# Cross-attention of a decoder layer: the next group's rows are normalised, turned and split during the output projection, and the batch turn runs in another order

## What is computed

```python
# H = 16 heads, DK = DV = 64, DIM = 512
q_i = _split_heads(q @ Wq, H)              # q = _layernorm(x)
k_i = _split_heads(k @ Wk, H)              # k = v = ctx_1024, (2, 128, 512)
v_i = _split_heads(v @ Wv, H)
s_qk = jnp.einsum('...hik,...hjk->...hij', q_i, k_i) / jnp.sqrt(DK)
s_qk = jnp.where(mask, s_qk, neg)
attn = jax.nn.softmax(s_qk, axis=-1)
vals = jnp.einsum('...hij,...hjv->...hiv', attn, v_i)
x = x + _merge_heads(vals) @ Wo
```

## Time and profile before

| | us |
|---|---|
| median of three runs (lowest, highest) | 2826.04 (2825.84, 2826.16) |
| the profiled execution, its own time | 2824.46 |
| its span in the trace | 2822.8 |
| PE busy in the span | 2761.5 (98%) |
| DVE, ACT, POOL busy in the span | 1783.8 (63%), 1592.6 (56%), 1063.0 (38%) |

### The profile page before, as it was taken

How to read it: one execution, slowest core, us unless ns; L and a number is a source line. 1 busy time by engine, 2 the same in 40 slices (tenths; PEclk the granted TensorE clock), 3 DMA queues, 4 the chain that set the end, 5 groups by cost and what they waited for, 6 DMA issues and landing times.

```text
span 2822.8 us, 46193 instructions
## 1 busy us (share of the span) xinstructions
PE 2761.5 (98%) x13287; PEld 2279.2 (81%) x13289; DVE 1783.8 (63%) x2600; ACT 1592.6 (56%) x2748; POOL 1063.0 (38%) x692
## 2 busy tenths in 40 slices
PE   7999999999999999999999999999999999999998
PEld 6888888888878888788778888887788888888886
DVE  6556565666876665667653333346795765677776
ACT  7888888888765554566621111112675644465665
POOL 6888888887622221122200000000342422333333
PEclk9999999999999999999999999999999999999999
DMA  1000000002231102110321111113896865787884
GB/s 64 27 27 11 26 26 26 11 30 63 83 98 46 45 30 90 39 37 27 112 93 63 60 59 59 59 59 111 323 355 211 326 217 166 257 299 239 294 288 174
DMA packets 191367, 326.90 MB, mean 116 GB/s; under 512 B 23592, under 2 KB 49192, under 8 KB 190784
## 3 DMA queue, kind: packets, MB, share of 16 engines
q1 hardware_dynamic: 180016, 300.81, 31.1%
q0 software_dynamic: 11280, 25.20, 2.6%
HBM read 288.95 MB, written 48.76 MB: 120 GB/s over the span
## 4 chain that ended last, share of the span: by engine, by line
PE 79%; issue 9%; DVE 5%; ACT 2%; POOL 2%; DMA 1%; ACTq 0%; DVEq 0%; POOLq 0%; SPq 0%
PE d_pG L1993 8%; PE d_pU L1993 8%; PE a_pS L47 4%; PE a_pS L49 4%; PE a_pS L48 4%; PE a_pO L47 4%; PE a_pO L49 4%; PE a_pO L48 4%; PE d_pD L49 3%; PE d_pD L47 3%; PE d_pD L48 3%; PE c_pD L49 2%; PE c_pD L47 2%; PE c_pG L47 2%; PE c_pD L48 2%
## 5 line engine op out<-in xcount | busy, mean ns | idle before, releaser
L158 POOL TENSOR_TENSOR a_pL<-a_p,a_pH 128x1024 fp32r<-128x1024 f32 x256 | 618.3, 2418 | 152.3 <-DVE a_p L345 149.9
L345 DVE TENSOR_TENSOR a_p<-a_r,a_pS 128x1024 f32<-128x1024 f32 x256 | 312.2, 1220 | 259.4 <-ACT a_r L166 254.2
L1229 DVE TENSOR_TENSOR e_wL<-e_raw,e_wH 128x1024 fp32r<-128x1024 f32 x384 | 450.1, 1217 | 33.8 <-PE d_pU L1993 23.1
L1224 ACT CAST e_wH<-e_raw 128x1024 fp32r<-128x1024 f32 x384 | 384.5, 1054 | 85.6 <-PE d_pD L49 59.5
L683 POOL TENSOR_TENSOR b_S<-b_S,b_ri 128x512 f32<-128x512 f32 x128 | 133.2, 1041 | 478.5 <-DVE b_ri L844 478.5
L166 ACT ACTIVATE a_r<-a_pS 128x1024 f32<-128x1024 f32 x256 | 261.8, 1023 | 78.8 <-PE a_pS L49 76.7
L166 ACT ACTIVATE a_pH<-a_r 128x1024 fp32r<-128x1024 f32 x256 | 271.9, 1062 | 9.1
L1473 POOL DMA_INDIRECT out<-d_og,c_iw x46 | 124.0, 2695 | 340.5 <-DVE d_og L1867 340.5
L700 ACT ACTIVATE b_S<-b_S,b_nm 128x128 f32<-128x128 f32 x512 | 198.9, 395 | 32.6 <-DVE b_nm L839 32.3
L47 PE MATMUL a_pS<-a_qH,a_kH 128*128 (+1 forms) x512 | 205.1, 401 | 2.3 <-DVE a_p L345 1.2
L47 PE MATMUL a_pO<-a_pH,a_vH 128*128 128x512 f32 x512 | 200.2, 391 | 1.5 <-POOL a_pL L158 1.5
(11 more groups left out here) (305 smaller groups left out, 7230.1 us busy)
## 6 DMA issues: line engine op xcount, KB each, us to landing
e_raw<-in_L_ffn_routed_gate_w SPq DMA_DIRECT2D x256, 256.0 KB, 4.6
e_raw<-in_L_ffn_routed_up_w SPq DMA_DIRECT2D x256, 256.0 KB, 5.7
e_raw<-in_L_ffn_routed_down_w SPq DMA_DIRECT2D x128, 512.0 KB, 6.6
a_xb<-in_x SPq DMA_DIRECT2D x8, 1024.0 KB, 5.5
x<-a_base SPq DMA_DIRECT2D x32, 256.0 KB, 2.3
b_xr<-x SPq DMA_DIRECT2D x32, 256.0 KB, 3.5
x<-b_xr SPq DMA_DIRECT2D x32, 256.0 KB, 3.0
c_xb<-x SPq DMA_DIRECT2D x32, 256.0 KB, 2.9
```

The source lines that it names most:

```text
L158: nc.gpsimd.tensor_tensor(pL[:, j % RING, :, :], p[:, j % 2, :, :], pH[:, j % RING, :, :].bitcast(F32), ALU.subtract).then_inc(s["low"], 1)
L345: v.tensor_tensor(p[:, j % 2, :, :], r[:, j % 2, :, :], pS[j % 2][:, :, :], ALU.mult).then_inc(s["p"], 1)
L1224: copy(self.wH[n][:, :, :], self.raw[n][:, :, :]).then_inc(self.s["high"], 1)
L1229: unit.tensor_tensor(self.wL[n][:, :, :], self.raw[n][:, :, :], self.wH[n][:, :, :].bitcast(self.F32), self.sub).then_inc(self.s["low"], 1)
```

## The change

The rows of groups 0 and 1 are handled as before. For groups 2 to 7:

- **PE**: `x_transpose` of tile i runs inside the projection in the group before: after `project(i)` for i = 0, 1, 2, and in the middle of `project(3)` for tile 3. All four go into `pQ`, one after the other; each waits until the low part of the tile before is written.
- **ACT**: the four `x_high` run at `j = 1`, after the second half of the exponentials.
- **DVE**: `x_low`, and `norm` of tiles 2 and 3, run between the additions of `outputs`; each statistic follows its own addition.
- **SP**: tiles 0 and 1 of the group after next are loaded at the end of a group's work; tiles 2 and 3 of the next group right after the first result is stored. The loop of batch 1 is written out on SP.
- **Batch turn**: PE runs `p_transpose(n - 1)` ahead of `scores(n)`, DVE the `inverse` of the pair before ahead of `add_mask`, and all seven parts of `row_scales` run in one piece at `j = 1` behind `outputs`.

```diff
+    pXQ = pQ[:, :].rearrange("p (a c) -> p a c", c=P)
+    def x_turned(g, i):
+        if isinstance(g, int) and g == 0:
+            return first_pX[i]
+        return pX[i % 2] if isinstance(g, int) and g == 1 else pXQ
...
+        def rows(g):
+            for i in range(2):
+                sp.wait_ge(s["normed"], g * GT + i - 1)
+                load(g * GT + i, i)
+        def more(g):
+            for i in range(2, GT):
+                sp.wait_ge(s["normed"], g * GT + GT + i - 1)
+                load(g * GT + GT + i, i)
-        def outputs(g):
+        def outputs(g, now, last):
             for i in range(GT):
                 reload(g, i)
                 if i:
                     store(g * GT + i - 1, i - 1)
+                if i == 1 and not last:
+                    more(now)
...
+            if not isinstance(g, int) or g + 2 < GROUPS:
+                rows(g + 2)
...
+                if j == 1 and not first and not last:
+                    for i in range(GT):
+                        x_high(g + 1, i)
...
-        def outputs(g):
+        def outputs(g, last):
             for i in range(GT):
+                if not last and i == GT - 1:
+                    x_low(g + 2, i)
                 add(g, i)
-                if i:
-                    out_stats(g, i - 1)
-            out_stats(g, GT - 1)
+                if not last and i < GT - 1:
+                    x_low(g + 2, i)
+                if not last and i < 2:
+                    norm(g + 2, i + 2)
+                out_stats(g, i)
...
+                turn = b > pb and j == 0
-                soon = b > pb and j == 0 or j >= NPAIR - 2 and last
+                soon = turn or j >= NPAIR - 2 and last
                 if soon:
                     t_low(n - 2)
+                if turn:
+                    inverse(n - 1, NPAIR - 1, 1)
                 add_mask(n, g, j)
...
-                if not last and j in X_SPLIT:
+                if first and j in X_SPLIT:
                     for i in range(2):
                         x_low(g + 1, 2 * X_SPLIT.index(j) + i)
-                if not last and j in X_NORM:
+                if j == 1 and not last or first and j == X_NORM[1]:
                     for i in range(2):
                         norm(g + 1, 2 * X_NORM.index(j) + i)
...
-                if b > pb and 1 <= j:
-                    row_scales(j - 1, KNOWN - GT, TILES)
+                if b > pb and j == 1:
+                    for part in range(len(SCALES_AT)):
+                        row_scales(part, KNOWN - GT, TILES)
...
         def x_transpose(t, i, g):
             pe.wait_ge(s["normed"], t + 1)
+            known = isinstance(g, int) and g <= 1
+            if not known:
+                wait(pe, s["qL"], NPAIR * (g - 1) + 4)
+                pe.wait_ge(s["xL"], t)
...
+                if j == 2 and not first and not last:
+                    pe.wait_ge(s["xL"], turn + GT)
...
+                if j or not first:
+                    p_transpose(n - 1, (j - 1) % NPAIR)
                 if early:
                     pe.wait_ge(s["k_in"], 64 * b)
                     scores(n, j)
-                if j or not first:
-                    p_transpose(n - 1, (j - 1) % NPAIR)
...
                     for i in range(GT):
-                        project(g - 1, i)
-                if not last and j in X_TURN:
+                        if last:
+                            project(g - 1, i)
+                        elif i < GT - 1:
+                            project(g - 1, i)
+                            x_transpose(turn + i, i, g + 1)
+                        else:
+                            project(g - 1, i, range(NPAIR // 2))
+                            x_transpose(turn + i, i, g + 1)
+                            project(g - 1, i, range(NPAIR // 2, NPAIR))
+                if first and j in X_TURN:
```

More of the change, by code:

```diff
@@ L550, in cross_attention, with groups @@
     X_NORM, X_TURN, X_SPLIT = (1, 3), (2, 4), (3, 5)
-    def groups(eng, body):
+    def groups(eng, body, loops=NB):
         for b in range(NB):
@@ L556, in groups @@
             end = (b + 1) * BG - (b == NB - 1)
-            with eng.Fori(b * BG + 1, end) as g:
-                body(g, b, b, False, False)
+            if b < loops:
+                with eng.Fori(b * BG + 1, end) as g:
+                    body(g, b, b, False, False)
+            else:
+                for g in range(b * BG + 1, end):
+                    body(g, b, b, False, False)
         body(GROUPS - 1, NB - 1, NB - 1, False, True)
@@ L647, in body @@
                         sp.dma_start(dst[row, :, i, :].bitcast(F32), part[row, :, :]).then_inc(s["k_in"], 16)
[L648 to L651, removed]
+            if first:
+                rows(g + 1)
             if b > pb:
@@ L655, in body @@
                     sp.dma_start(dst[:, 0, :, :, :].bitcast(F32), part).then_inc(s["mv_in"], 16)
[L656 to L662, removed]
+            if first:
+                more(g)
+            else:
+                outputs(g - 1, g, last)
+            if not isinstance(g, int) or g + 2 < GROUPS:
+                rows(g + 2)
+        groups(sp, body, 1)
         ending(reload, store, free)
@@ L688, in x_high @@
             act.wait_ge(s["xt"], g * GT + i + 1)
-            source = first_pX[i] if isinstance(g, int) and g == 0 else pX[i % 2]
+            source = x_turned(g, i)
             nc.scalar.activation(x_part(xH, g, slice(0, KC), slice(i * P, (i + 1) * P)), source, ACT.Copy).then_inc(s["xH"], 1)
@@ L962, in body @@
                     t_low(n - 2)
-                if j or not first:
+                if (j or not first) and not turn:
                     inverse(n - 1, (j - 1) % NPAIR, 1)
@@ L981, in body @@
                 if j == 1 and not first:
-                    outputs(g - 1)
+                    outputs(g - 1, last)
                 if j == NPAIR - 1 and not last:
@@ L1001, in x_transpose @@
             pe.wait_ge(s["normed"], t + 1)
[L1002 to L1008, removed]
+            known = isinstance(g, int) and g <= 1
+            if not known:
+                wait(pe, s["qL"], NPAIR * (g - 1) + 4)
+                pe.wait_ge(s["xL"], t)
+            elif g == 1 and i >= 2:
+                pe.wait_ge(s["xL"], t - 1)
+            out, source = x_turned(g, i), xn0 if known and g == 0 else xn
             for c in range(KC):
@@ L1124, in body @@
                 elif not last:
-                    if j == NPAIR - 2:
+                    if first and j == NPAIR - 2:
                         pe.wait_ge(s["xL"], turn + GT)
```

## The result

Over 22 runs of each the changed kernel takes **2821.1 us** (2818.41 to 2823.24) and the kernel before 2825.88 us (2824.89 to 2827.91). The ratio is 0.9982, 95% interval 0.9977 to 0.9988: a gain of 4.8 us, 0.18%, clear of zero and on the border of the 0.2% that was named. The forecast was 2820.5.

The account below looks back on a forecast made before the run. PE, busy 98% of the span, was taken as the bound, with DVE's delays going straight into it. Terms -6.1 - 0.1 + 0.9 - 0.2 = -5.5 us gave a median of 2820.5 us, 8-in-10 range 2818.0 to 2825.5.

Parts of the forecast that it names:

- Steady periods: Cross-attention periods 1 to 6: 3.06 us of PE time removed from pairs, 1.84 added in the projection, net -1.22 us each.
- the hand-over: Single accumulator pQ passing PE, ACT, DVE, PE for each tile: 2.0 to 2.3 us, taken to cause no wait.
- The batch turn: End of period 3, new order of PE and DVE: DVE's chain sets the pace, -0.1 us.
- The row scales in one piece: Period 4: 4.7 us of DVE work, 4.4 idle on PE, 1.55 for the slow clock; period +0.9 us.
- extras of 0.38: Row scales on DVE: an extra 0.38 us read behind some aggregates; without them the piece takes 4.3 us.
- The last group: Last group of cross-attention: order kept but for the statistics, -0.2 us.
- rival 1: Period 4: the slow clock has no price; -7.0 us in all, 2819.0 us; chance 0.14.
- rival 2: The clock falls both at the batch turn and in period 4: -3.9 us, 2822.1 us; chance 0.10.
- rival 3: Late x_low(2) or rows hold PE up about 0.5 us a period: -2.5, 2823.5 us; 0.15 together with rival 5.
- rival 4: Residual rows come late and PE waits in project(3): +6 us, 2832 us, slower; chance 0.06.
- rival 5: Pairs have another bound than 6.44 us, half the steady gain stays: -2.5 us; 0.15 together with rival 3.
- the term of +0.9: Period 4 with row scales in one piece: 81.55 us against 80.62 before.

Follow-up runs that it names:

- Experiment 7: The changed kernel with tile 3 turned right behind tile 2, ahead of project(3) instead of in its middle: 2833.37 us, ratio 1.0024 to the kernel before.
- Experiment 3: The changed kernel with the old order at the batch turn, scores ahead of p_transpose and inverse behind add_mask: 2821.4 us, ratio 0.9987 to before.
- experiment 6: The changed kernel with row_scales ahead of outputs and batch 1's keys loaded in two halves, the first early: 2811.72 us, ratio 0.9950 to before.
- experiment 2: The changed kernel with row_scales spread again, one part at each j from 1 to 7: 2818.08 us, ratio 0.9976 to before.
- Experiments 1: The changed kernel with all seven parts of row_scales ahead of outputs at j = 1 of group 4: 2815.52 us, ratio 0.9964 to before.
- experiment 4: The changed kernel with parts 0 to 3 of row_scales ahead of outputs and parts 4 to 6 behind it: 2816.64 us, ratio 0.9973 to before.
- experiment 10: The changed kernel as it is, run again on another comparison's chip: 2821.5 us, ratio 0.9986 to the kernel before.

## Why the prediction was right

**Steady periods.** Forecast -1.22 us each, measured -1.12 to -1.33. The mechanism was right: DVE's extras at j = 2, 3 and 5 went one to one into PE, and in the cover they cost nothing: from j = 2 to j = 0 the pairs of period 2 lost 3.1 us, forecast 3.06, with each pair within 0.02 us of its forecast. A turn of a tile inside the projection costs slightly more than forecast: projection and four turns take 957.89 - 934.07 = 23.82 us in period 2, so (23.82 - 21.86) / 4 = 0.49, not 0.46. Together that is -3.1 + 1.96 = -1.1, as measured in period 2. Experiment 7 shows that the hand-over was sized rightly, too.

**The batch turn.** Forecast -0.1; the trace has 17.26 us from the query of j = 0 to the projection (1089.37 - 1072.11), against 17.31. Experiment 3 gives 0.02 us for the order, experiment 6 shows its bound. DVE's chain does set the pace in the new order: `values(31)` starts 14.97 us after the query of j = 0, where 14.8 to 14.9 was forecast. In the kernel before it did not: PE runs from 1083.91 to the projection at 1092.30 without a wait, 8.39 us of its own work, slow in part. The forecast took the difference of the two rightly, but that it is so near to nothing is chance, since the two orders have different bounds. The idle pieces were 1.41 and 1.5 us, the second shorter than the 1.9 forecast, and the clock stayed.

**The row scales in one piece.** Forecast 4.7 us of DVE, 4.4 of PE, 1.55 of the clock. Measured 4.34 of DVE: none of the extras of 0.38 occurred. They had been no part of the piece. In the kernel before, `add_mask` at 1124.17 starts 0.38 us after the last `scores` matmul has, and so it does at 1139.44, where the view names PE:

```profile
1123.79 0.28 PE L49 MATMUL b_pS<-b_kH,b_qL 128*128 128x256 f32 x1
...
1139.06 0.28 PE L49 MATMUL b_pS<-b_kH,b_qL 128*128 128x256 f32 x1
1139.44 1.22 DVE L833 TENSOR_TENSOR b_S<-b_pS,b_bias 128x1024 f32<-128x1024 f32 x1 [0.35 <-PE b_pS L49]
```

So the row that the prediction read as the price of an aggregate was a wait for `scores`; in experiment 2, where `scores` are over earlier, `add_mask` follows the same four aggregates after 0.04 us. The rule of the Trainium skill (VectorE: DVE Perf Modes, "The DRAIN you can't avoid"), by which the semaphores behind such instructions cost nothing beyond their spacing, was right here against my reading of that row. PE reached `values` 4.14 us late (1121.49, against 1113.17 + 1.43 + 2.75), where 4.4 was forecast. The clock cost 1.5 to 1.6: `values` and the transposes took 3.82 us (1125.31 - 1121.49), 2.16 at the full clock, of which 0.1 is the first matmul's start. Period 4: forecast 81.55, measured 81.45. Experiments 1 and 4 show both prices.

**The last group.** Forecast -0.2, measured -0.3.

**The sum.** -5.1 in the periods and -0.3 behind them, -5.4 in all, against -5.5 forecast. The medians say -4.8 and -4.0 in the two comparisons, less than the traces of cross-attention. Stretches of slow clock elsewhere, as in experiment 10, are large enough for such a difference; that they make it is not shown. The profiled execution was forecast at 2819.0 and took 2819.78, 0.7 of it from the offset ahead of cross-attention, and it stood 1.3 below its median, not 1.58. That the median came within 0.6 us of the forecast is in part luck: executions of one kernel spread by 3 to 5 us.

**Rivals.** The clock fell in period 4 (not rival 1) and not at the turn (not rival 2). Neither the hand-over (rival 3) nor the residual rows (rival 4) held PE up: landing of `xr` had a median of 2.6 us and a largest of 8.9, but that was not in a steady projection. Pairs do run at 6.44 (not rival 5).

What I had seen and not followed up: the term of +0.9 had a free alternative in the same profile. DVE stands idle for 7.45 us before the first addition in that very projection, for its residual rows:

```profile
1101.13 0.69 DVE L858 TENSOR_TENSOR b_xr<-b_pY,b_xr 128x512 f32<-128x512 f32 x1 [7.45 <-DMA b_xr<-x]
```

## What to carry to other kernels

Where a second engine's chain in a step is as long as the bound engine's step, each instruction on it costs its length; look for the phase in which the bound engine works alone, and put there all that has no deadline in the step. But put it ahead of that phase's own last deadline: the same 4.3 us cost nothing before the additions and 5.7 us after them. When an order of instructions removes a visible wait, ask first what chain runs beside it, and whether the new order sets that chain back: at the batch turn a 2 us wait and a slow clock went away, DVE's chain came 0.5 us later, and the period stayed the same to 0.02 us.

## What the runs showed of the hardware that was not expected

- A slow stretch costs less than its length says when another engine's chain runs beside it. In experiment 3 the granted clock was 0.51 for 3.4 us, and transposes, scores and query took 6.20 us (1087.26 - 1081.06) for some 4.7 at the full clock (0.4, 1.5 and 2.75). By the estimate from its rows 0.9 of these 1.5 us reached the period, and the rest lay under DVE's chain.
- The length of an idle piece alone did not decide whether the clock fell. The same kernel had the same wait of 2.97 us in two executions (changed and experiment 10) and the granted clock behind it was 1.00 in one and 0.55 in the other. In cross-attention waits of 1.44 us (experiment 4), 1.53 (the turn of the changed kernel) and 1.51 to 1.85 (experiment 7) were not followed by the lower level, those of 2.08, 2.09, 2.10 and 3.98 us were.
- Small DVE instructions that wait for each other follow at 0.20 us in one piece, and at 0.20 to 0.27 where they are spread between larger instructions (experiment 2). The 0.38 behind an aggregate in the earlier trace rows is a wait for PE's scores. One other gap, 0.40 us behind the last part (before `add_mask` at 1157.14 in experiment 2, and in the kernel before), has no cause that the traces show.
